# Graph attention and a mixture of experts on one core: the mean of rows without edges as a bias, diagonal tiles and rows on ScalarE, and the last block's routing over more engines

## The reference

```python
x = x + gnn(layernorm(x), adj)        # x is (8192, 128), adj (8192, 8192) of int32
x = x + moe(layernorm(x))             # 16 experts, top 2, hidden 256
# gnn: h = n @ W.T + b_W
#   e = leaky_relu((h @ a1)[:, None] + (h @ a2)[None, :] + b_a, 0.2)
#   softmax over the columns where adj > 0, else -9e15;  result = attention @ h
# moe: logits = n @ gate_w + gate_b; the two best, weights renormalised to 1
#   y = sum over both of  weight * (silu(n @ w1[e]) * (n @ w2[e])) @ w3[e]
```

## Time and profile before

| | |
|---|---|
| median of 3 runs | 1827.13 us (1823.32 to 1829.69) |
| the profiled execution, its own time | 1837.41 us |
| its span | 1835.6 us |
| its mean granted clock | 0.958 |
| busy: PE, DVE, ACT, POOL | 1532.3, 1469.1, 1279.2, 600.1 us |
| from 1450 to 1530 us: PE's busy time | 4.7 us |
| HBM | 309.57 MB read, 28.51 MB written |

### The profile page before, as it was taken

The page is one execution under the profiler, slowest core; times in us unless marked ns, Lnnn a source line. Parts: engine busy times, 40 slices in busy tenths (PEclk is TensorE's granted clock), DMA queues, the critical chain, the costliest instruction groups (busy, mean ns, idle before and its releaser), DMA issues.

```text
span 1835.6 us, 24897 instructions
## 1 busy us (share of the span) xinstructions
PE 1532.3 (83%) x8112; PEld 845.5 (46%) x8113; DVE 1469.1 (80%) x2024; ACT 1279.2 (70%) x1620; POOL 600.1 (33%) x840
## 2 busy tenths in 40 slices
PE   5587798898899889988988998899999605999991
PEld 5454344454344435444543444445555303666660
DVE  7789899989989998999899999988977412444444
ACT  4889798788869887987888688867765302555550
POOL 6500110230424133213604231341332563555551
PEclk9999999999999999999999999999999857999995
DMA  6899687667738774876577387635423114222227
GB/s 193 293 325 306 211 263 245 202 195 241 239 112 281 240 219 136 272 234 195 187 253 239 117 279 243 219 98 162 148 60 120 38 35 144 74 72 75 72 75 285
DMA packets 119651, 339.40 MB, mean 185 GB/s; under 512 B 16962, under 2 KB 39682, under 8 KB 119426
## 3 DMA queue, kind: packets, MB, share of 16 engines
q1 hardware_dynamic: 104528, 303.26, 51.9%
q0 software_dynamic: 11824, 28.50, 4.8%
q10 hardware_dynamic: 3202, 6.38, 1.0%
HBM read 309.57 MB, written 28.51 MB: 184 GB/s over the span
## 4 chain that ended last, share of the span: by engine, by line
PE 36%; DVE 33%; issue 15%; POOL 8%; ACT 5%; DMA 3%; SPq 0%; ACTq 0%; another core or an unknown queue 0%; DVEq 0%; POOLq 0%
PE pair L899 17%; DVE probs L1209 15%; DVE ring L1155 13%; PE pair L986 7%; PE pair L886 5%; PE pair L1002 3%; ACT ring L691 3%; PE pair L993 2%; DMA ring<-res_d 1%; POOL xd_d L605 1%; ACT probs L742 1%; PE pair L982 1%; POOL ln L566 1%; POOL numT L575 1%; POOL xd_d L658 1%
## 5 line engine op out<-in xcount | busy, mean ns | idle before, releaser
L899 PE MATMUL pair<-probs,X 128*128 128x512 f32 x2048 | 1016.6, 614 | 0.1
L742 ACT ACTIVATE probs<-probs,ebias 128x1024 f32<-128x1024 f32 (+1 forms) x576 | 602.1, 1047 | 273.6 <-DVE probs L1209 267.5
L1209 DVE SCALAR_TENSOR_TENSOR probs<-s1row,ns,pair 128x1024 f32<-128x1024 f32 (+1 forms) x576 | 656.7, 1154 | 73.9 <-PE pair L886 60.7
L1155 DVE CUSTOM_DVE_ANT_0 ring<-urow,ring 128x2048 int8<-128x2048 f16 x256 | 594.7, 2325 | 10.7 <-ACT ring L691 10.7
L691 ACT ACTIVATE ring<-stage,neghalf 128x1024 int8<-128x1024 int32 x512 | 574.5, 1140 | 1.8 <-DMA stage<-in_adj 1.5
L886 PEld LDWEIGHTS pair<-diag,ring 128*128 128x128 fp8e5 x4096 | 265.1, 99 | 496.5 <-DVE probs L1209 274.5
L886 PE MATMUL pair<-diag,ring 128*128 128x128 bf16 x4096 | 328.3, 221 | 153.8 <-DVE probs L1209 128.1
L899 PEld LDWEIGHTS pair<-probs,X 128*128 128x128 f32 x2048 | 348.4, 193 | 218.1 <-issue 216.5
L663 POOL DMA_INDIRECT res_d<-probs x144 | 139.0, 965 | 134.3 <-ACT probs L790 127.8
L1430 DVE COPY probs<-pair 128x256 f32<-128x256 f32 x144 | 61.1, 424 | 140.4 <-PE pair L993 84.5
L605 POOL DMA_INDIRECT xd_d<-xres,sloti x128 | 158.1, 1235 | 40.0 <-issue 33.5
(11 more groups left out here) (217 smaller groups left out, 838.0 us busy)
## 6 DMA issues: line engine op xcount, KB each, us to landing
stage<-in_adj SPq DMA_DIRECT2D x512, 512.0 KB
probs<-xd_d SPq DMA_DIRECT2D x144, 65.0 KB
ring<-res_d SPq DMA_DIRECT2D x16, 512.0 KB, 9.9
ring<-in_L_ffn_w SPq DMA_DIRECT2D x2, 2048.0 KB, 12.1
ring<-xmid_d SPq DMA_DIRECT2D x1, 4096.0 KB
out<-ring ACTq DMA_DIRECT2D x8, 512.0 KB, 6.9
xres<-in_x POOLq DMA_DIRECT2D x7, 512.0 KB, 7.2
s1row<-s_d SPq DMA_DIRECT2D x7, 512.0 KB, 6.8
```

What stands on the lines that cost most here:

```text
L742: act.activation(probs[:, n % PR, 0:wide], probs[:, n % PR, 0:wide], ACT.Exp, bias=ebias[:, j:j + 1], scale=RISE).then_inc(probs_ready, 1)
L899: m = pe.matmul(acc[q][:, lo:hi], X[:, j, :], probs[:, n % PR, lo:hi], start=(j == 0), stop=(j == NT - 1))
L1155: dve.tensor_tensor_reduce(m, urow[:, c * CH:(c + 1) * CH], m, CODE, NO_EDGE, ALU.subtract, ALU.max, part[:, k, c:c + 1]).then_inc(piece_d ...
L1209: dve.scalar_tensor_tensor(out=probs[:, n % PR, 0:wide], in0=s1row[:, q, 0:wide], scalar=ns2[:, j:j + 1], in1=Tp[n % 2][:, 0:wide], op0=AL ...
```

## The change

**Rows without edges.** The accumulated sums get a tiny bias, `xtiny` = 2^-64 times the column sums of the normalised rows, when ScalarE copies them to SBUF (`ACT.Identity` with a bias). Where a row has edges the bias vanishes in rounding; where it has none, numerator and denominator are both the tiny one and their quotient is the mean. `noedge`, `den`, `nshare`, `mean_row`, `mean_product` and the two GpSimd operations that used them go.

**Work moved between engines.** `make_diag` and the normalising of rows go from GpSimd to ScalarE. For blocks 0 to 6 (`by_act`) ScalarE also scales the projected rows by `rden` into `numT`, and GpSimd adds them to x in one operation; for blocks 7 and 8 VectorE still does both as before.

**Block 7's routing** is drawn forward in block 8 so that all of it lies in the 64 steps. GpSimd's preparation of the empty rows and of some constants, which stood between block 7's norm and its scatter, goes ahead of block 7's store (`prepare`).

**The last block** gets routines of its own: `last_norm` on VectorE alone (the steps of `finish`, four statistics, then 24 short operations, of which 16 follow each other by links, three Newton steps among them; no wait for GpSimd), the counts and the weights on VectorE (the lines after `top_two` below, with three short operations for the two weights), the store on SP, two copies of the normalised rows on ScalarE (so that the eight scatters follow each other without a wait for the first four), and the empty rows' 16 writes on SP and ScalarE, eight each, as plain DMAs with addresses read from SBUF. SP reads the table before it waits for the scatters.

In the diff, `prepare`, `store_xmid` and `scatter_last` are GpSimd's, `make_diag`, `normal_rows`, `scaled_rows` and `last_rows` ScalarE's; the lines from `last_norm()` on are VectorE's.

```diff
-        return dict(stats=36, per=1, root=50, top=56, ranks=NT, slots=NT, weights=NT)
+        return dict(stats=26, per=2, root=32, top=38, ranks=46, slots=48, weights=51)
+    def project_at(host, r):
+        return 8 + 14 * r if host < NB - 1 else 8 + 7 * r
+    def finish_at(host, r):
+        return 11 + 13 * r if host < NB - 1 else 10 + 7 * r
...
+        def by_act(b):
+            return b < NB - 2
+        def pad_rows(engine, kind, experts):
+            n = len(experts)
+            r = nc.values_load_multi_w_load_instructions(
+                pad_i[0:1, experts[0]:experts[0] + n], engines=(kind,), min_val=0, max_val=(E - 1) * CAP + N,
...
+            for i, e in enumerate(experts):
+                engine.dma_start(xd_d[bass.ds(r[i], P), :], pads[:, e, :]).then_inc(pad_out, 16)
...
+            sp.wait_ge(proj_read, ROUND0[NB])
+            sp.dma_start(xmid_t[:, ROW0[LAST]:NT, :], xres[:, LQ, 0:LN, 0:D]).then_inc(last_out, 16)
+            sp.wait_ge(pad_ready, 1)
+            pad_rows(sp, mybir.EngineType.SP, range(E // 2))
             sp.wait_ge(prod_done, NT * NB)
+            sp.wait_ge(tab_ready, 1)
+            r = rows_of(0, XS)
             for c in range(2):
                 sp.wait_ge(disp[c], 16 * NT)
-            sp.wait_ge(tab_ready, 1)
             sp.wait_ge(pad_out, 16 * E)
-            r = rows_of(0, XS)
...
+            def store_xmid(b):
                 pool.wait_ge(proj_read, ROUND0[b + 1])
-                pool.tensor_tensor(share, mean_row[:, 0:D].unsqueeze(1).to_broadcast([P, n, D]),
-                                   nshare[:, 0:n].unsqueeze(2).to_broadcast([P, n, D]), ALU.mult
-                                   ).then_inc(share_ready, 1)
+                if by_act(b):
+                    pool.wait_ge(xres_in[q], 16 * (b // 2 + 1))
+                    pool.tensor_tensor(rows, rows, share, ALU.add).then_inc(xmid_ready, 1)
+                    pool.wait_ge(xmid_ready, b + 1)
                 pool.dma_start(xmid_t[:, ROW0[b]:ROW0[b + 1], :], rows).then_inc(xmid_out, 16)
...
-                pool.tensor_tensor(t2, per_e(mean_row[:, D + 1:GW], b), per_t(nshare[:, 0:n], b), ALU.mult)
-                plink(pool.tensor_tensor(lg, pgs[:, 0:n, :], cols[:, ROW0[b]:ROW0[b + 1], 2:2 + E], ALU.add))
-                plink(pool.tensor_tensor(lg, lg, t2, ALU.add))
+                pool.tensor_tensor(lg, pgs[:, 0:n, :], cols[:, ROW0[b]:ROW0[b + 1], 2:2 + E], ALU.add)
...
+            def scatter_last():
+                pool.wait_ge(rows_ready, NB)
+                pool.wait_ge(wr_ready, NB)
+                pool.wait_ge(slot_ready, NB)
+                for c in range(2):
+                    for k in range(LN):
+                        pool.indirect_dma_start(
+                            out=xd_d[:, :], out_offset=bass.IndirectOffsetOnAxis(ap=sloti[:, LQ, c, k:k + 1], axis=0),
+                            in_=xres[:, LQ, c * LN + k, :], in_offset=None).then_inc(disp[c], 16)
...
+            for b in range(LAST):
+                if b == LAST - 1:
+                    prepare()
+                store_xmid(b)
+                norm_rows(b)
+                gate_logits(b)
+                destinations(b, 0)
                 for c in range(2):
                     scatter(b, c)
...
+            def make_diag(b):
+                act.wait_ge(c_ready, b + 1)
+                for k in range(BLOCKS[b]):
+                    ins = act.activation(diag[:, q, k, :], ident[:, :], ACT.Copy, scale=cdiag[:, k:k + 1])
+            def normal_rows(b, k):
+                if k == 0:
+                    act.wait_ge(norm_ready, b + 1)
+                    act.wait_ge(xmid_out, 16 * (b + 1))
+                ins = act.activation(xres[:, q, k, 0:D], xres[:, q, k, 0:D], ACT.Identity,
+                                     bias=ln2[:, 5, k:k + 1], scale=ln2[:, 4, k:k + 1])
+            def scaled_rows(b, r, i):
+                if i == 0:
+                    act.wait_ge(den_ready, ROUND0[b] + r + 1)
+                ins = act.activation(numT[:, k * P:(k + 1) * P], acc[q][:, at:at + D], ACT.Copy,
+                                     scale=rden[:, k:k + 1])
...
+                    if b >= 1 and by_act(b - 1):
+                        for r in range(ROUNDS[b - 1]):
+                            i = j - (finish_at(b, r) + 2)
+                            if 0 <= i < min(4, BLOCKS[b - 1] - 4 * r):
+                                scaled_rows(b - 1, r, i)
+                    if b >= 1:
+                        k = j - route_units(b)["top"]
+                        if 0 <= k < BLOCKS[b - 1]:
+                            normal_rows(b - 1, k)
+                    if b + 1 < NB and j == CHAIN_AT + 2:
+                        make_diag(b + 1)
...
+            act.wait_ge(norm_ready, NB)
+            last_rows(1)
+            act.wait_ge(last_out, 16)
+            last_rows(0).then_inc(rows_ready, 1)
+            weights(LAST)
+            act.wait_ge(pad_ready, 1)
+            pad_rows(act, mybir.EngineType.Activation, range(E // 2, E))
...
+            last_norm()
+            for step in range(TOPS):
+                top_two(LAST, step)
+            rlink(dve.tensor_reduce(ohred[:, :], ohb[:, 0:LN * E].rearrange("p (t e) -> p e t", e=E), AX.X, ALU.add))
+            dve.tensor_tensor(ohall[:, 0:E], ohsum[:, 0:E], ohred[:, :], ALU.add).then_inc(all_ready, 1)
+            dve.wait_ge(we_ready, NB)
...
+            for step in (0, 1, 2, 4):
+                slots(LAST, step)
```

More of the change, by code:

```diff
@@ L149, in graph_moe_layer @@
         cdiag = sb("cdiag", [P, TMAX])
-        noedge = sb("noedge", [P, TMAX])
-        den = sb("den", [P, TMAX])
         rden = sb("rden", [P, TMAX])
-        nshare = sb("nshare", [P, TMAX])
         neghalf = sb("neghalf", [P, 1])
@@ L377, in graph_moe_layer @@
         ROUND0 = [sum(ROUNDS[:b]) for b in range(NB + 1)]
+        def by_act(b):
+            return b < NB - 2
+        LAST, LQ, LN = NB - 1, (NB - 1) % 2, BLOCKS[NB - 1]
+        assert 2 * LN <= TMAX and ROUNDS[LAST] == 1
+        def pad_rows(engine, kind, experts):
+            n = len(experts)
+            r = nc.values_load_multi_w_load_instructions(
+                pad_i[0:1, experts[0]:experts[0] + n], engines=(kind,), min_val=0, max_val=(E - 1) * CAP + N,
+                skip_runtime_bounds_check_because="an expert has at most as many rows as there are tokens")[1]
+            for i, e in enumerate(experts):
+                engine.dma_start(xd_d[bass.ds(r[i], P), :], pads[:, e, :]).then_inc(pad_out, 16)
         block = ctx.enter_context(nc.Block())
@@ L653, in _ @@
                 if b + 2 < NB:
-                    load_xres(b + 2)
-            pool.wait_ge(pad_ready, 1)
-            for e in range(E):
-                pool.indirect_dma_start(
-                    out=xd_d[:, :], out_offset=bass.IndirectOffsetOnAxis(ap=pad_i[:, e:e + 1], axis=0),
-                    in_=pads[:, e, :], in_offset=None).then_inc(pad_out, 16)
+                    load_x(b + 2)
+            scatter_last()
             for i in range(ST):
@@ L766, in _, with last_rows @@
                         numerators(b - 1)
+                    if b >= 1 and by_act(b - 1):
[7 more added lines that the diff above has]
+                            normal_rows(b - 1, k)
                     if b >= 1 and j == route_units(b)["slots"]:
                         weights(b - 1)
[L769 to L772 removed]
+                    if b + 1 < NB and j == CHAIN_AT + 2:
+                        make_diag(b + 1)
+            numerators(LAST)
+            def last_rows(c):
+                for k in range(LN):
+                    ins = act.activation(xres[:, LQ, c * LN + k, 0:D], xres[:, LQ, k, 0:D], ACT.Identity,
+                                         bias=ln3[:, 6, k:k + 1], scale=ln3[:, 4, k:k + 1])
+                return ins
+            act.wait_ge(norm_ready, NB)
[5 more added lines that the diff above has]
+            pad_rows(act, mybir.EngineType.Activation, range(E // 2, E))
             def copy_xsT(i, v, first):
@@ L894, in product @@
                 pe.wait_ge(probs_ready, n + 1)
+                if j == 0 and b == 1:
+                    pe.wait_ge(mean_ready, 1)
                 if j == 0 and b >= 2:
@@ L1232, in finish @@
                         dve.wait_ge(lg_ready, b)
-                    flink(dve.tensor_scalar(pairs(noedge), dens, 0.0, None, ALU.is_equal))
+                    flink(dve.reciprocal(pairs(rden), dens))
                 elif step == 1:
                     dve.wait_ge(fin, fins[0])
-                    flink(dve.scalar_tensor_tensor(out=pairs(den), in0=pairs(noedge), scalar=mean_row[:, D:D + 1],
-                                                   in1=dens, op0=ALU.mult, op1=ALU.add))
-                elif step == 2:
-                    dve.wait_ge(fin, fins[0])
-                    flink(dve.reciprocal(rden[:, w], den[:, w]))
-                elif step == 3:
-                    dve.wait_ge(fin, fins[0])
```

(17 more changed lines are left out.)

243 lines of the change are left out of this document (138 added, 105 removed).

## The result

The changed kernel takes 1751.55 us (median of 4 runs, 1749.56 to 1751.89); the kernel before took 1828.41 us in the same sitting (4 runs). The ratio is 0.958, with a 95% interval of 0.955 to 0.960: 76.9 us less, against 73.7 forecast (1753 us). The profiled execution took 1749.56 us, span 1747.8, clock 0.976.

The account below looks back on a forecast made before the run. VectorE was taken to bound blocks 1 to 6, TensorE blocks 7 and 8, GpSimd's queue the stretch behind them. 14.6 + 4.0 + 1.7 + 1.2 + 0.9 + 51.3 = 73.7 us off 1827.13 gave 1753.4, range 1742 to 1772.

Parts of the forecast that it names:

- Part 1: VectorE in blocks 1 to 6: rows and short operations leave it, 2.66 us a block, 1.3 in block 1, 14.6 us.
- Part 2: Gate chain: VectorE waits less for GpSimd's last gate operation, 0.7 us in five blocks, 0.5 in block 1, 4.0 us.
- Part 3: GpSimd's addition holds VectorE's maxima 1.1 us in five blocks instead of 1.8 in four, gain 1.7 us.
- Rival (c): GpSimd's addition holds the maxima in full in five blocks, 1.8 us each: 3.5 us more, 1756.9 us; chance 0.1.
- Part 4: Diagonal tiles on ScalarE: 1.2 us gained at the start, 0.9 at the change from block 0 to block 1.
- Part 5: Block 7's routing inside block 8: its sixteen writes end near 1456.5 us instead of 1475.16; ranks cost some 1.3 us.
- Part 6: Last block up to the experts: they start at 1478.6 us, 51.3 us earlier, between 45 and 56.
- (a): Blocks do not get shorter because another engine takes VectorE's place: parts 1 to 3 fall away, 1773.7 us; chance 0.1.
- (d): ScalarE becomes the bound of the blocks and the kernel gets slower than before, 1857 us; chance 0.02.
- (b): Block 7's routing slips out of block 8; the last eight writes start 10 us later, 1763.4 us; chance 0.08.

Follow-up runs that it names:

- moves_taken_back: Changed kernel with rows of all blocks back on VectorE, diagonal tiles and normalising of blocks 0 to 7 back on GpSimd: 1773.98 us, ratio 0.963.
- block7_routed_late: Changed kernel with block 7's routing and finish back at their old steps, the empty rows' preparation staying ahead of block 7's store: 1760.93 us, ratio 0.963.
- after_again: The changed kernel, unchanged, traced again on one chip in one sitting with the kernel before: 1761.49 us, ratio 0.960.
- scalar_rows_twice: Changed kernel with ScalarE executing each scaled and each normalised row once more into an unread scratch tile: 1752.35 us, ratio 0.958.

## Why the prediction was right, point by point

**Part 1 (14.6 us).** Right: the rows 2.06 us a block, forecast 2.1; the three short operations twice, 0.52 by the difference between before and moves_taken_back, forecast 0.5. Block 1 gave 1.30. Together 14.2. The bounds were summed wrongly, without effect on the result: the best cases given for parts 1 to 4 add to about 41 us, not 36. ScalarE's new work at nothing held, with room for 16 of its 24 operations once more.

**Part 2 (4.0 us).** Mechanism right, size too small: 1.05 in each of five blocks and 0.68 in block 1, 5.9. The step that failed is "between nothing and the whole 1.35 I take half"; the wait shrank by the 1.01 us that the chain lost, since VectorE stood there with nothing else to do.

**Part 3 (1.7 us).** The number holds by luck, its working does not. Before, five maxima were held by GpSimd's addition (462.81, 631.28, 800.08, 968.52 and 1137.05, each 4.08 or 4.09 us), not four; and after it five are held for 1.23 us each, not 1.1. That gives 0.57 a block, 2.9 us; from it go 1.0 us for another maximum of four blocks that now takes 2.54 us where it took 2.28. The remedy, one wait, was worth 6.2 us by its trace, over three times the part. Rival (c), full holding, did not come.

**Part 4 (2.1 us).** In the kernel before TensorE got its first tiles at

```profile
96.20 1.03 PE L886 MATMUL pair<-diag,ring 128*128 128x128 bf16 x8 [21.82 <-POOL diag L509]
```

and in the changed one 1.23 us earlier (95.71, in a trace that ran 0.74 us late until then), forecast 1.2; the change to block 1 gave 1.03 by its own run, forecast 0.9. More came at both places (the table's 3.7 and 2.7 us), and their cause is not shown. In block 0 alone, traces of the same code differ from the changed kernel's by up to 2.7 us, and in one case by 7.1, so the table's 3.7 is within that scatter.

**Part 5.** GpSimd was free far ahead of time (17.52 us of waiting for the weights), and its last write ended 7.9 us behind the last product, forecast 7.6 (1456.5 less 1448.9). The 1.3 us for the ranks inside the steps held as well: from the last maximum to the last product the changed kernel takes 97.9 us, block7_routed_late, whose ranks lie behind the steps, 96.8. (The trace of before has 98.3 there, with the loss that goes with the sitting in it.) Against that, ScalarE's copy no longer stands 2.5 us behind the last product to wait for block 7's slots. The margin of GpSimd before the last block's first write was 6.3 us, not 8.7, because VectorE was quicker than forecast.

**Part 6 (51.3 us).** From the copy of the last sums to the experts 29.1 us, forecast 29.7, by two misses that cancel. Forecast and measured from that copy: last row finished 4.5, 3.5; gate logits 9.8, 8.4; the ohb operation's end 13.2, 11.5; slots 15.8, 13.4; first write 16.3, 14.2; last issue 25.2, 23.1. Against it the last issue to the experts' start: 4.5 forecast, 6.08 measured, and 7.4 in after_again. The step that failed is that the empty rows' DMAs land "near 1472, hidden behind the scatter": the last landed at 1440.2, 11.5 us after the first issue and not 6.5, 0.8 us ahead of the last write, and they delayed it. Of the 50.8 us by which this stretch got shorter between the first two traces, runs take back two pieces, 18.6 us for the empty rows and 7.5 for block 7's routing. The remaining 25 (the norm on VectorE alone, the eight writes without a wait between, the store on SyncE) are read from the traces; no run takes them back one by one.

**Rivals.** (a) and (d) are refuted by the block of 163.4 us and by scalar_rows_twice. (b) did not occur; when it was forced the time rose by 9.4 us against its 10, with some luck: the writes started 10.6 us later, but landed 1.8 us sooner. The forecast of 165 us for a block was 1.6 too long, 1.1 of it by the trace of before, whose blocks held the loss that goes with the sitting.

## What to carry to other kernels

Where a large operation on one engine holds one on another (here 1.2 to 1.8 us each time), the order of their starts can be worth more than the split of the work (1.24 against 0.83 us a block): move the large operation behind the held one, into a stretch where the other engine reads PSUM. In an uncovered tail, count each queue's issues and landings apart: plain DMAs on idle queues save issue time, but their packets delay the last write (4.05 instead of 2.30 us). And before a difference between two traces is put down to the code, trace both kernels on the same chip in the same sitting.

## What was not expected of the hardware

ScalarE's 128x128 operation takes 350 ns with one column operand from PSUM (L807) and 479 with two from SBUF (L784), more than the 368 of the earlier trace rows. VectorE lost 1.0 to 1.6 us, once up to 2.6, at each block change from the third on in five traces and nothing in nine others; twice, code that was the same in the blocks stands on both sides.
